# Routing weights of the gated experts as two fp16 parts laid out four times, and spread for two inner blocks at once from the two halves of the rows

## The reference, cut to what matters

```
scores  = sigmoid(h @ gate_w.T);  the best 4 of 8 groups, then the best 8 experts of them
combine = weights of the chosen experts / their sum * 2.5      # [token, 32], zero elsewhere
g = silu(einsum('th,eih->tei', h, w_gate));  u = einsum('th,eih->tei', h, w_up)
routed = einsum('tei,ehi->th', g * u * combine[:, :, None], w_down)
shared = silu(h @ sh_gate.T) * (h @ sh_up.T) @ sh_down.T
f = routed + shared
```

## Time and profile before

| what | value |
|---|---|
| median of 3 runs (lowest to highest) | 3316.39 us (3313.81 to 3322.95) |
| the profiled execution, its own time | 3321.88 us |
| its span in the trace, mean granted TensorE clock | 3320.1 us, 0.908 |
| TensorE busy | 2796.0 us, 84% of the span |
| VectorE busy | 2213.3 us, 67% |
| ScalarE busy | 1846.6 us, 56% |
| GpSimd busy | 1484.9 us, 45% |
| experts' inner blocks (layer 0) in the trace | 1404.2 to 1720.0 us |
| routing and projection (out0) ends | about 1393 us |

### The profile page before, as it was taken

The page is one execution under the profiler, slowest core; times in us unless marked ns, Lnnn a source line. Parts: engine busy times, 40 slices in busy tenths (PEclk is TensorE's granted clock), DMA queues, the critical chain, the costliest instruction groups (busy, mean ns, idle before and its releaser), DMA issues. The chain is left out here.

```text
span 3320.1 us, 67732 instructions
## 1 busy us (share of the span) xinstructions
PE 2796.0 (84%) x21369; PEld 1304.9 (39%) x21370; DVE 2213.3 (67%) x3341; ACT 1846.6 (56%) x3190; POOL 1484.9 (45%) x1112
## 2 busy tenths in 40 slices
PE   5999999999999996899974499999996942476994
PEld 2333333333333333733333122222225942364772
DVE  5666666566666662988886799999982347535663
ACT  4555555555555552154455299999993654255432
POOL 1899999999999996400000011110112535441000
PEclk7999999999999997999996599999998975587995
DMA  2111111111111112600003312112214670262002
GB/s 81 32 50 43 57 44 44 50 43 53 49 44 50 43 47 88 225 1 1 0 2 112 75 41 51 44 44 50 45 40 146 189 211 28 67 180 58 11 13 57
DMA packets 275318, 208.27 MB, mean 63 GB/s; under 512 B 148846, under 2 KB 210726, under 8 KB 274320
## 3 DMA queue, kind: packets, MB, share of 16 engines
q1 hardware_dynamic: 266992, 192.77, 20.4%
q0 software_dynamic: 8224, 14.24, 1.3%
HBM read 125.43 MB, written 66.77 MB: 58 GB/s over the span
## 5 line engine op out<-in xcount | busy, mean ns | idle before, releaser
L604 DVE TENSOR_REDUCE attn_half_max<-attn_peek 128x2 f32<-128x1024 f32 x504 | 617.8, 1226 | 452.0 <-PE attn_peek L415 448.2
L353 POOL TENSOR_TENSOR attn_esum<-attn_esum,attn_prob 128x1024 f32<-128x1024 f32 x384 | 904.3, 2355 | 30.5 <-ACT attn_prob L521 4.6
L521 ACT ACTIVATE attn_prob<-attn_score 128x1024 f32<-128x1024 f32 x512 | 512.5, 1021 | 299.0 <-PE attn_score L389 297.0
L914 ACT ACTIVATE attn_prob<-attn_score 128x512 f32<-128x512 f32 x1024 | 556.3, 596 | 73.0 <-PE attn_score L864 58.9
L931 DVE TENSOR_REDUCE attn_half_max<-attn_peek 128x2 f32<-128x1024 f32 x512 | 583.7, 1217 | 11.0 <-PE attn_peek L850 11.0
L447 PE MATMUL attn_acc<-attn_prob,attn_v 128*64 128x512 f32 x2048 | 489.0, 599 | 0.1
L880 PE MATMUL attn_acc<-attn_prob,attn_v 128*32 128x256 f32 x4096 | 328.3, 392 | 12.1 <-ACT attn_out L906 10.6
L1803 POOL DMA_INDIRECT sorted_x<-attn_sent_rows,attn_send x64 | 62.5, 976 | 555.8 <-PE attn_score L864 555.8
L850 PE MATMUL attn_peek<-attn_ke,attn_qe 48*128 48x512 bf16 x1024 | 203.0, 393 | 45.0 <-DMA attn_ke<-k 30.0
L447 PEld LDWEIGHTS attn_acc<-attn_prob,attn_v 128*64 128x64 f32 x2048 | 131.2, 137 | 208.0 <-issue 163.5
L864 PE MATMUL attn_score<-attn_qe,attn_ke 49*128 49x512 bf16 x1024 | 200.8, 389 | 8.4 <-ACT attn_prob L914 5.5
(11 more groups left out here) (552 smaller groups left out, 4299.5 us busy)
## 6 DMA issues: line engine op xcount, KB each, us to landing
experts_w<-in_L_ffn_W SPq DMA_DIRECT2D x80, 256.0 KB
attn_xb<-attn_x_all SPq DMA_DIRECT2D x64, 256.0 KB, 2.6
attn_invB<-inv SPq DMA_DIRECT2D x64, 256.0 KB
o<-attn_out SPq DMA_DIRECT2D x32, 512.0 KB, 2.7
out_o<-o SPq DMA_DIRECT2D x8, 2048.0 KB
experts_w<-in_L_ffn_w SPq DMA_DIRECT2D x40, 256.0 KB
mix_f<-picked SPq DMA_DIRECT2D x16, 512.0 KB, 7.3
experts_x<-sorted_x SPq DMA_DIRECT2D x112, 65.0 KB
```

What stands on the lines that cost most here:

```text
L353: nc.gpsimd.tensor_tensor(own, before, prob[:, u % NPROB, :, :], ALU.add).then_inc(added, 1)
L521: nc.scalar.activation(prob[:, u % NPROB, :, :], score[:, u % 2, :, :], ACT.Exp).then_inc(exped, 1)
L604: V.tensor_reduce(half_max[:, :, t, half], first_look(m) if first else peek[:], AX.X, ALU.max, negate=True).then_inc(maxed, 1)
L914: nc.scalar.activation(prob[:, n % NPROB, :], score[:, n % RING, :], ACT.Exp).then_inc(exped, 1)
```

## The change

- `split_weights` scales by 2^10 and writes a high and a low fp16 part, and one more copy repeats both: `parts` is now [tile, copy, part, expert] with 2 x 2 x 32 = 128 columns in place of 96. Five VectorE instructions become three. The transposes and the copies to `gated_cT` keep their number and have 128 rows.
- `select` builds four groups of 32 rows in place of three: eight selects in place of six.
- In the experts' stage GpSimd copies the chunk's 128 x 512 piece of `cT` into `here` (two slots), one copy per chunk.
- `rep` has three PSUM buffers. TensorE computes `rep` for blocks k and k+1 ahead of the matmuls of an even block k, with two matmuls: rows 0 to 63 of `sel` and `here` for block k, rows 64 to 127 for block k+1. Each has 64 rows. They wait for `brought` (the copy) at k = 0 and for `mixed` of block k-2. The single 96-row matmul between `up[1]` and `down` is gone, and `second_up` is raised by the last `up[1]` matmul.
- VectorE reads `rep[:, k % 3]` and divides by 2^10 in the same instruction as before.

```diff
-        parts = st.sb("parts", [P, NT, PARTS, E], BF16)
+        parts = st.sb("parts", [P, NT, 2, 2, E], F16)
...
             def split_weights():
-                link(V.tensor_copy(parts[:, :, 0, :], pick[:]))
-                link(V.tensor_tensor(tmp[:], pick[:], parts[:, :, 0, :], ALU.subtract))
-                link(V.tensor_copy(parts[:, :, 1, :], tmp[:]))
-                link(V.tensor_tensor(tmp[:], tmp[:], parts[:, :, 1, :], ALU.subtract))
-                V.tensor_copy(parts[:, :, 2, :], tmp[:]).then_inc(parts_ready, 1)
+                high, low = parts[:, :, 0, 0, :], parts[:, :, 0, 1, :]
+                link(V.tensor_scalar(high, pick[:], gated.SHARE_SCALE, None, ALU.mult))
+                link(V.scalar_tensor_tensor(out=low, in0=pick[:], scalar=gated.SHARE_SCALE, in1=high, op0=ALU.mult, op1=ALU.subtract))
+                V.tensor_copy(parts[:, :, 1, :, :], parts[:, :, 0, :, :]).then_inc(parts_ready, 1)
...
-        for part in range(3):
+        for part in range(self.COPIES):
...
+        @block.gpsimd
+        def _(pool):
+            def body(i, slot, first):
+
+                if not (isinstance(i, int) and i < 2):
+                    pool.wait_ge(spread_out, i - 1)
+                nc.gpsimd.tensor_copy(here[:, slot, :], cT[:, bass.ds(i * CH, CH)]).then_inc(brought, 1)
...
+            def spread(i, slot, k, first):
+
+                if k == 0:
+                    pe.wait_ge(brought, i + 1)
+                if not (first and k < 2):
+                    pe.wait_ge(mixed, i * HT + k - 1)
+                for m in (k, k + 1):
+                    half = slice(m % 2 * P // 2, (m % 2 + 1) * P // 2)
+                    last = nc.tensor.matmul(rep[:, m % 3, :], sel[half, m * P:(m + 1) * P], here[half, slot, :], start=True, stop=True)
+                if k == NSEL - 2:
+                    last.then_inc(spread_out, 1)
...
+                    if k % 2 == 0 and k < NSEL:
+                        spread(i, slot, k, first)
                     if not (first and k < 2):
                         pe.wait_ge(acted, n - 1)
                     product(up[0][:, s, :], up_w[0], own, x_parts, (slice(None), tok), True, True).then_inc(first_up, 1)
                     if not (first and k < 2):
                         pe.wait_ge(mixed, n - 1)
-                    ins = product(up[1][:, s, :], up_w[1], own, x_parts, (slice(None), tok), True, True)
-                    if k < NSEL:
-                        ins = nc.tensor.matmul(rep[:, s, :], sel[:, own], cT[:, tok], start=True, stop=True)
-                    ins.then_inc(second_up, 1)
+                    product(up[1][:, s, :], up_w[1], own, x_parts, (slice(None), tok), True, True).then_inc(second_up, 1)
```

More of the change, by code:

```diff
@@ L1070, in project_and_route_stage @@
     E = 32
-    PARTS = 3
     with Stage(nc, "out0") as st:
@@ L1078, in project_and_route_stage @@
         score, pick, tmp = (st.sb(n, [P, NT, E]) for n in ("score", "pick", "masked"))
-        parts = st.sb("parts", [P, NT, PARTS, E], BF16)
-        ident16 = st.sb("ident16", [P, P], BF16)
+        parts = st.sb("parts", [P, NT, 2, 2, E], F16)
+        ident16 = st.sb("ident16", [P, P], F16)
         best = st.sb("best", [P, NT, 8])
@@ L1090, in project_and_route_stage @@
         turned_w = st.ps("turned_w", [P, E])
-        trb = st.ps("trb", [PARTS * E, 2, 8, P], BF16)
+        trb = st.ps("trb", [P, 2, 8, P], F16)
         job = beside(st)
@@ L1141, in turn_weights @@
                         pe.wait_ge(b_copied, t // 8 - 1)
-                    last = nc.tensor.transpose(trb[:, t // 8 % 2, t % 8, :], parts[:, t, :, :].rearrange("p a e -> p (a e)"), ident16[:])
+                    last = nc.tensor.transpose(trb[:, t // 8 % 2, t % 8, :], parts[:, t, :, :, :].rearrange("p c a e -> p (c a e)"), ident16[:])
                     if t % 8 == 7:
@@ L1489 @@
     NSEL = 16
+    COPIES = 4
+    SHARE_SCALE = 2.0 ** 10
     def __init__(self, ctx, nc, weights):
@@ L1494, in __init__ @@
         self.raw = ctx.enter_context(nc.sbuf_tensor("gated_raw", [P, 3, self.HT, P], F32))
-        self.cT = ctx.enter_context(nc.sbuf_tensor("gated_cT", [96, TOK], BF16))
-        self.sel = ctx.enter_context(nc.sbuf_tensor("gated_sel", [96, self.NSEL * P], BF16))
+        self.cT = ctx.enter_context(nc.sbuf_tensor("gated_cT", [P, TOK], F16))
+        self.sel = ctx.enter_context(nc.sbuf_tensor("gated_sel", [P, self.NSEL * P], F16))
         self.powers = ctx.enter_context(nc.sbuf_tensor("gated_powers", [P, SsmPowers.KEPT, SEQ], F32))
@@ L1544, in gated_experts_stage @@
         h_parts = [st.sb(f"h{part}", [P, 2, CH], F16) for part in range(2)]
+        here = st.sb("here", [P, 2, CH], F16)
+        brought, spread_out = st.sem("brought"), st.sem("spread_out")
         a = st.sb("a", [P, 2, CH])
@@ L1548, in gated_experts_stage @@
         up = [st.ps(f"up{n}", [P, 2, CH]) for n in range(2)]
-        rep = st.ps("rep", [P, 2, CH])
+        rep = st.ps("rep", [P, 3, CH])
         acc = st.ps("acc", [P, CH])
@@ L1585, in _ @@
             sp.wait_ge(gated.stored, SsmPowers.STORES * DMA)
+        @block.gpsimd
[4 more added lines that the diff above has]
+                nc.gpsimd.tensor_copy(here[:, slot, :], cT[:, bass.ds(i * CH, CH)]).then_inc(brought, 1)
+            iterations(pool, body)
         @block.tensor
@@ L1721, in body @@
                         dve.wait_ge(tmp_ready, i * NSEL + k + 1)
-                    V.scalar_tensor_tensor(out=h[:, s, :], in0=(rep if k < NSEL else up[1])[:, s, :], scalar=H_SCALE / UP,
+                    V.scalar_tensor_tensor(out=h[:, s, :], in0=rep[:, k % 3, :] if k < NSEL else up[1][:, s, :],
+                                           scalar=H_SCALE / (UP * gated.SHARE_SCALE) if k < NSEL else H_SCALE / UP,
                                            in1=(g if k < NSEL else a)[:, s, :], op0=ALU.mult, op1=ALU.mult).then_inc(mixed, 1)
```

## The result

The changed kernel takes 3331.94 us in the median of 8 runs (3328.07 to 3336.91); the kernel before, with 8 runs, 3318.62 us. The two medians are 13.3 us apart. The ratio is 1.0038, 95% interval 1.0029 to 1.0048, which is 12.6 us slower (9.6 to 15.9); the text goes by this ratio. The profiled execution took 3331.64 us, its span is 3329.6 us. The forecast was 12.4 us more, 3329 against the median known then.

What follows compares the result with a forecast made beforehand. The prediction took a ring between TensorE and VectorE in the experts' stage as the bound. Stage +10.6, out0 +0.8 and GpSimd's copies +1.0 sum to +12.4 us, from the 3316.4 median to 3329 us, range 3315 to 3341.

Steps and rivals of the forecast that it cites:

- The ring: Experts' stage: TensorE and VectorE wait on each other, fixed delay 2.55 us plus nine matmul starts, 4.50 us per two blocks.
- The removed slot: Experts' stage: the rep matmul saved per pair of blocks reappears as a 0.38 us wait at the odd block's down matmul.
- the spread: Experts' stage: the two 64-row rep matmuls per pair of blocks, claimed to add 0.41 us to TensorE's queue.
- The halves run side by side: Experts' stage: both 64-row rep matmuls share one slot; rival, one after the other, 12.1 us more, 3341, chance 0.08.
- the change of form: Experts' stage: TensorE going between 128*128 and 64*128 matmuls, twice per pair of blocks, 0.095 us each.
- the likeliest rival: Experts' stage: changing rows alone costs nothing, leaving +1.8 us from out0 and the copies, 3318 us; chance 0.16.
- the full tail of a matmul: Experts' stage, rival: each change of form drains TensorE fully, 0.16 us, adding 18.5 us, in all 3337; chance 0.12.
- The stage: Experts' stage: 0.19 us more per pair of blocks, seven pairs in each of eight chunks, +10.6 us.
- out0: Stage with the weight split on VectorE: split grows from 6.3 to 7.1 us, +0.8 (-1.3 to +2.1).
- GpSimd's copies: Experts' stage: copies of 0.3 to 1.2 us each, off the path, but slowing VectorE's low part of h, +1.0 us.
- Slower by over 0.3%: Whole kernel: outcome given 0.58, from two thirds of the forecast's 0.58 and the two costlier rivals' 0.20.
- the rival "faster": Experts' stage: g starts earlier, two blocks fall to VectorE's 4.33 us, 11 us less, 3305; chance 0.06.

Runs made afterwards that it cites:

- early raise: The kernel before, with second_up raised by the last up matmul and rep raising a semaphore of its own: ratio 0.9967, two blocks in 4.33 us.
- full rows: The changed kernel with rep as two 128-row matmuls one after the other in place of the 64-row halves: ratio to before 1.0057.

## Why the prediction was right

- **The ring bounds the stage**: shown by the early raise (4.33 us per pair with all instructions kept) and by leaving `rep` out (no better). The delay from g to the down matmul is 2.08 us before and after, and g starts 0.48 behind the last up matmul (1499.25, five steps behind 1498.17) where it started 0.47 behind `rep`.
- **The removed slot comes back as a wait**: shown. The pair grew although one slot went; the odd block's down matmul waits 0.39 us (2.76 less nine slots and the spread's 0.42) where 0.38 was forecast.
- **The halves run side by side, the change of form costs about 0.095**: the step into the 64-row form is 0.31, as forecast, the step out 0.32 against 0.31. The spread adds 0.42 (0.41 forecast), the pair is 4.71 (4.69 forecast). Leaving the form alone and paying a whole slot (full rows) costs the same pair. The change is not free for rows alone, which was the likeliest rival. The loss per change, 0.10, is also well short of the full tail of a matmul, 0.16, with which a pair would have taken 4.83. The Trainium skill, TensorEngine Tiling (Array Packing), Key Properties, says that a change of tiling mode drains TensorE; the trace agrees that a change costs time, and the full tail was my reading of it, an estimate that the trace does not bear out.
- **The stage**: 11.3 us longer, 10.6 forecast. Each pair pays 0.21 and not 0.19, in 54 pairs and not 56, since the first two of the first chunk lose nothing. The last three blocks of a chunk take 6.85 us against 6.84: the wait there took the cost up, as forecast.
- **out0**: +0.8 forecast, 7.43 - 6.27 = +1.2 measured. The sum sized the subtraction and the copy with their stretch by the selects too low, at 4.7 together: they took 2.79 and 2.27.
- **GpSimd's copies**: 0.61 us each in the median, within 0.3 to 1.2. They do stretch the low part, by 0.3 to 0.4 us each, 2.1 in all, so the reading was right and more than the +1.0 of the sum. But all six fall in the last pair of a chunk (k = 14 and 15), where TensorE waits anyway. In the chunks with a copy that pair has blocks of about 2.12 and 2.17 us, in the last two chunks, without one, 1.95 and 2.34: 4.29 both times. What failed in this term is where the stretch falls: it was put on the ring and lies beside it, so the term was too high by 1.0.
- **Sum**: 12.4 forecast, 11.3 + 1.2 = 12.5 by the traces, 12.6 by the ratio. The terms for the stage and for out0 were too low by 0.7 and 0.4, the one for the copies too high by 1.0. That the sum is right to 0.1 us is luck: the misses cancel, and the stages that were not edited vary by more than that.
- **Slower by over 0.3%** was given 0.58; the ratio is 1.0038, and its interval begins at 1.0029, so that it is only just on that side.
- **Slips in the working**: the rival "faster" left the +1.8 for out0 and the copies out of its sum, which gives 3307 and not 3305. "Faster" has 0.08 at the end where its only rival has 0.06, and "same" 0.34 where its parts give 0.35. The forecast hangs on neither.

## What to carry to other kernels

Before removing work from the busiest engine, follow one item around all engines: if the signal that leaves it, the other engines' delay and the wait that takes the item back make a ring longer than the engine's own work, less work between the signal and the wait only lengthens that wait, and moving the signal one instruction forward (no work removed) is what pays. Two changes of form cost 0.2 us here, as much as the one 512-column matmul that a single pair of halves saves. More pairs of halves standing together would share that cost; this was not tried here. A slowed instruction costs time only where it sets the pace: GpSimd's copies stretched VectorE in the one pair of a chunk that had time to spare, and cost nothing. Where a PSUM bank is free, look first at which wait in the trace a second buffer would end.

## What the runs showed of the hardware

- A change between 128*128 and 64*128 alone costs 0.096 us on the way in (0.312 against steps of 0.216) and 0.10 on the way out (0.318), at a granted clock of 1.00. With 128 rows at the same place (full rows) both steps are 0.216. Going from 96 rows to 128 costs next to nothing (0.220).
- Three VectorE instructions with all operands in SBUF took 2.38, 2.79 and 2.27 us while GpSimd's selects ran; the bf16 cast of the same size takes 0.69 alone. Beside GpSimd's fp16 copies the low part took 0.97 to 1.07 us in place of 0.68, while h, which reads PSUM, kept its 0.69.
- In the kernel without `rep`, TensorE stood still six times in layer 1's attention, a stage that was not edited. First this kernel, then the kernel before at the same matmul:

```profile
2001.82 0.64 PE L880 MATMUL attn_acc<-attn_prob,attn_v 128*32 128x256 f32 x8
2005.62 0.61 PE L864 MATMUL attn_score<-attn_qe,attn_ke 49*128 49x512 bf16 x2 [3.16 <-issue]
```
```profile
2013.02 0.39 PE L864 MATMUL attn_score<-attn_qe,attn_ke 49*128 49x512 bf16 x2 [0.38 <-ACT attn_prob L914]
```

  The step at this matmul is 3.3 to 3.8 us in place of 0.75 (which all the other eleven profiles show), and "issue" means that the profile shows nothing it waited for. The six are 768 matmuls apart, each at the first matmul after one of the six jumps back of this stage's loop (seven turns). Behind each pause the granted clock fell. Windows views of that kernel (granted clock third from the end):

```profile
2002.70:2005.40 2.70, 0.00 (x0) 0.00 (x0) 1.01 (x1) 0.08 (x1) 0.00 (x0) 1.00 0.20 61
2005.50:2012.00 6.50, 6.38 (x40) 1.22 (x40) 3.68 (x3) 3.77 (x7) 0.00 (x0) 0.50 0.31 91
```
```profile
1950.00:2050.00 100.00, 93.81 (x962) 26.27 (x960) 93.42 (x91) 88.81 (x166) 9.78 (x10) 0.97 0.18 42
```

  And of the kernel before:

```profile
1950.00:2050.00 100.00, 96.64 (x1024) 28.13 (x1020) 98.45 (x96) 94.12 (x176) 10.75 (x11) 1.00 0.19 43
```

  With TensorE idle for about 3 us ahead of it, the clock went from 1.00 to 0.50 (1.2 GHz, the lower of its two levels), for 6.8 us after five of the pauses and 3.4 after the last. A turn of the loop so took 80.3 us and not 75.2, 29 us in all, of which the pauses themselves are 17. Why TensorE paused is open. The values that pass through the stage are others, since the experts' weights were left out, and the program ahead of the stage is shorter, so that its loop lies elsewhere in it; no run tells these two apart. It is a warning: a kernel that leaves a computation out can be slower as a whole for a reason outside the work left out, and should be read by its stage.
